# Finer projection parts, placed by a table around the row pieces of a causal attention stage

## The reference

```
q = concat(heads(x @ Wq1), heads(x @ Wq2))     # 16 + 16 heads of 32 columns, two inputs x [1024, 512] each
k2, v2 = repeat(heads(x @ Wk), 2), repeat(heads(x @ Wv), 2)
p = softmax(where(causal, q @ k2.T / sqrt(32), min))
y1, y2 = split(p @ v2)
x = x + (y1 - sigmoid(x @ Wlam) * y2) @ Wo
```

## Time and profile before

| what | value |
|---|---|
| median of 3 runs | 2034.17 us (2033.46 to 2034.27) |
| the profiled execution | 2035.76 us |
| its span, first to last instruction | 2034.0 us |
| everything ahead of the attention's prologue | 0 to about 760 us |
| attention prologue | 760 to 815 us |
| units 0 to 15 | 815 to 1669 us |
| last feed-forward layer | 1669 to 2034 us |
| TensorE busy over the span | 1962.1 us, 96% |
| VectorE, GpSimd, ScalarE busy over the span | 64%, 42%, 41% |

### The profile page before, as it was taken

The page is one execution under the profiler, slowest core; times in us unless marked ns, Lnnn a source line. Parts: engine busy times, 40 slices in busy tenths (PEclk is TensorE's granted clock), DMA queues, the critical chain, the costliest instruction groups (busy, mean ns, idle before and its releaser), DMA issues.

```text
span 2034.0 us, 36832 instructions
## 1 busy us (share of the span) xinstructions
PE 1962.1 (96%) x15143; PEld 834.2 (41%) x15184; DVE 1305.1 (64%) x2610; ACT 827.7 (41%) x1259; POOL 864.2 (42%) x451
## 2 busy tenths in 40 slices
PE   7898999899999999999999999999998899899999
PEld 3444444444444443333333333333333334344444
DVE  5878686846847456566666666666667635774644
ACT  4435353425444322444434443344434452543431
POOL 3756576700000000667677667777776740000000
PEclk9999999999999999999999999999999999999999
DMA  8111010030000003000101010010000211000001
GB/s 243 32 31 33 30 42 27 21 140 1 1 1 1 1 1 76 23 17 23 22 22 22 12 26 14 22 23 22 2 22 6 60 36 42 1 1 22 21 0 42
DMA packets 71592, 60.21 MB, mean 30 GB/s; under 512 B 37312, under 2 KB 55744, under 8 KB 71168
## 3 DMA queue, kind: packets, MB, share of 16 engines
q1 hardware_dynamic: 64512, 45.27, 8.0%
q10 hardware_dynamic: 6912, 12.59, 2.0%
HBM read 43.02 MB, written 10.62 MB: 26 GB/s over the span
## 4 chain that ended last, share of the span: by engine, by line
PE 53%; DVE 5%; POOL 2%; issue 1%; ACT 1%; DVEq 0%; POOLq 0%; ACTq 0%
PE psum L128 9%; PE psum L1231 8%; PE psum L1321 8%; PE psum L1379 6%; PE psum L1362 6%; PE psum L152 5%; PE psum L1271 3%; PE psum L1335 2%; PE psum L1358 2%; POOL b_totals L1628 1%; PE psum L1349 1%; DVE b_maxima L1701 1%; PE psum L1280 1%; DVE psum L1709 1%; DVE x L1767 0%
## 5 line engine op out<-in xcount | busy, mean ns | idle before, releaser
L1628 POOL TENSOR_TENSOR b_totals<-b_totals,b_probs 128x2048 f32<-128x2048 f32 (+3 forms) x100 | 323.9, 3239 | 151.7 <-ACT b_probs L1546 148.1
L1709 DVE CUSTOM_DVE_ANT_0 psum<-psum,b_rest 128x512 f32<-128x512 f32 (+3 forms) x512 | 233.7, 526 | 172.2 <-PE psum L1321 172.0
L447 PE MATMUL psum<-hT,a_win 128*128 128x512 f32 x640 | 292.9, 601 | 2.6 <-DVE a_parts L751 1.2
L128 PE MATMUL psum<-hT,b_early 128*128 128x512 f16 x1024 | 227.2, 381 | 9.8 <-DVE b_middle L214 6.9
L128 PE MATMUL psum<-hT,W 128*128 128x512 f16 x1024 | 227.5, 382 | 3.7 <-DVE a_win L214 3.6
L1546 ACT ACTIVATE b_probs<-psum 128x1024 f32<-128x1024 f32 (+3 forms) x214 | 153.6, 768 | 150.5 <-PE psum L1362 150.4
L1701 DVE TENSOR_REDUCE b_maxima<-psum 128x2 f32<-128x1024 f32 x128 | 150.9, 1221 | 86.0 <-PE psum L1321 85.7
L1628 POOL TENSOR_TENSOR b_totals<-b_totals,b_rest 128x2048 f32<-128x2048 f32 (+3 forms) x50 | 161.9, 3238 | 68.3 <-ACT b_rest L1546 66.6
L447 PEld LDWEIGHTS psum<-hT,a_win 128*128 128x128 f32 x640 | 120.2, 192 | 130.8 <-issue 129.5
L128 PEld LDWEIGHTS psum<-hT,b_early 128*128 128x128 bf16 x1024 | 100.0, 98 | 133.8 <-DVE b_middle L214 8.8
L128 PEld LDWEIGHTS psum<-hT,W 128*128 128x128 bf16 x1024 | 100.7, 99 | 126.4 <-issue 7.0
(11 more groups left out here) (244 smaller groups left out, 3476.6 us busy)
## 6 DMA issues: line engine op xcount, KB each, us to landing
a_parts<-in_w_guT ACTq DMA_DIRECT2D x32, 256.0 KB, 2.7
ternary<-W SPq DMA_DIRECT2D x1, 6144.0 KB, 18.3
a_win<-in_w_inT SPq DMA_DIRECT2D x20, 256.0 KB, 7.9
a_parts<-in_w_pT ACTq DMA_DIRECT2D x16, 256.0 KB, 2.6
b_down<-lam_rows SPq DMA_DIRECT2D x32, 128.0 KB, 2.7
b_early<-ternary SPq DMA_DIRECT2D x8, 512.0 KB, 8.9
out<-x SPq DMA_DIRECT2D x16, 256.0 KB, 2.3
x<-in_x SPq DMA_DIRECT2D x3, 1024.0 KB, 8.0
```

What stands on the lines that cost most here:

```text
L128: last = pe.matmul(self.bank[self.up_bank(i, m) + part], self.gu[:, k * 2 * HID + col:k * 2 * HID + col + P], self.hT[:, at:at + BLK], sta ...
L447: last = pe.matmul(ring(s, j), win[:, at:at + P], core["hT"][:, (i * KT + k) * BLK:(i * KT + k + 1) * BLK], start=(k == 0), stop=(k == KT ...
L1628: pool.tensor_tensor(acc, acc, held(u, s)[:, :, off:BLK], ALU.add).then_inc(summed, 1)
L1709: last = dve.tensor_tensor_reduce(scores, scores, row_mask[:, BLK - width:BLK], 1.0, -3e38, ALU.add, ALU.max, maxima[u % 2][:, at:at + 1])
```

## The change

1. A "k" or "q" job now has 8 parts of half the width: the parts 0 to 3 do the first 256 token columns over the four input blocks, the parts 4 to 7 the other 256. A "v" job also has 8 parts, of 4 matmuls where it had 4 of 8. A unit with four jobs has 32 parts, of half the size.
2. A step has 6 places in place of 2. Places 0 and 1 come ahead of the rows, 2 to 5 behind. Two tables say how many parts stand in a step, `AHEAD_OF_ROWS` and `BEHIND_ROWS`. The sums over the next chunk of queries move: "den1" from behind the rows of step 2 to ahead of the rows of step 3, "den0" to place 3 of step 5, which is behind one part of a projection.
3. The row pieces stand in another order.
4. In unit 14, where "norm" jobs take the place of the projections, all four stand behind the rows; the one of step 4 stood ahead.

```diff
-ROWS = [[(0, 0), (2, 0)], [(4, 0)], [(1, 0), (5, 1)], [(5, 0)], [(6, 0)], [(4, 1), (6, 1)], [(3, 0)], [(7, 1)], [(7, 0)]]
+ROWS = [[(4, 0)], [(5, 0)], [(0, 0), (2, 0)], [(1, 0), (5, 1)], [(3, 0)], [(4, 1), (6, 1)], [(6, 0)], [(7, 1)], [(7, 0)]]
...
-PARTS = {"k": KT, "q": KT, "v": KT}
+PARTS = {"k": 2 * KT, "q": 2 * KT, "v": 2 * KT}
 
-FIRST_HALF = {(0, 0): "k0", (2, 1): "den1", (3, 0): "k1", (5, 1): "den0", (6, 0): "q0", (8, 0): "q1", (10, 1): "neg0"}
-SECOND_HALF = {(0, 0): "q0", (2, 1): "den1", (3, 0): "q1", (5, 1): "den0", (6, 0): "v0", (8, 0): "v1", (10, 1): "neg0"}
+MADE_IN = [("k0", "k1", "q0", "q1"), ("q0", "q1", "v0", "v1")]
+AHEAD_OF_ROWS = {4: 2, 5: 1, 6: 1, 7: 1, 8: 1}
+BEHIND_ROWS = {0: 2, 1: 3, 2: 3, 3: 1, 4: 3, 5: 1, 6: 3, 7: 3, 8: 3, 9: 4}
+PLACES = 6
+FILLS = []
+for _names in MADE_IN:
+    _halves = [(i, first + n) for i in range(NS) for first, table in ((0, AHEAD_OF_ROWS), (2, BEHIND_ROWS))
+               for n in range(table.get(i, 0))]
+    FILLS.append({at: _names[n // (2 * KT)] for n, at in enumerate(_halves)})
+    FILLS[-1].update({(3, 0): "den1", (5, 3): "den0", (10, 2): "neg0"})
...
-FILL_BEFORE_ROWS = (0, 4)
-NORM_AT = {(3, 0): 0, (4, 0): 1, (6, 0): 2, (7, 0): 3}
+NORM_AT = {(3, 2): 0, (4, 2): 1, (6, 2): 2, (7, 2): 3}
...
-            def project(weights, r, c, k, to):
-                at = ((r // HT * CQ + c) * KT + k) * BLK
+            def project(weights, r, c, part, to):
+                k, width = part % KT, BLK // 2
+                first = part // KT * width
+                at = ((r // HT * CQ + c) * KT + k) * BLK + first
                 for own in COLUMNS:
-                    last = pe.matmul(to[own, :], weights[:, k * P + own.start:k * P + own.stop], hT[:, at:at + BLK],
-                                     start=(k == 0), stop=(k == KT - 1))
+                    last = pe.matmul(to[own, first:first + width], weights[:, k * P + own.start:k * P + own.stop],
+                                     hT[:, at:at + width], start=(k == 0), stop=(k == KT - 1))
...
-                    if i in FILL_BEFORE_ROWS and (u, i, 0) in PART_AT:
-                        fill(*PART_AT[u, i, 0])
-                    if row_in(u, i):
-                        row(*row_in(u, i))
-                    if i not in FILL_BEFORE_ROWS and (u, i, 0) in PART_AT:
-                        fill(*PART_AT[u, i, 0])
-                    if (u, i, 1) in PART_AT:
-                        fill(*PART_AT[u, i, 1])
+                    for place in range(PLACES):
+                        if place == 2 and row_in(u, i):
+                            row(*row_in(u, i))
+                        if (u, i, place) in PART_AT:
+                            fill(*PART_AT[u, i, place])
```

More of the change, by code:

```diff
@@ L1 @@
+import itertools
 from contextlib import ExitStack
@@ L940, in job_from @@
         return {(1, 1): ("den", u - 1, 1), (4, 0): ("den", u, 0)}.get((i, place))
-    name = (SECOND_HALF if w else FIRST_HALF).get((i, place), "none0")
+    name = FILLS[w].get((i, place), "none0")
     kind, n, last = name[:-1], int(name[-1]), r == TURNS - 1
@@ L964 @@
 EPILOGUE_BANKS = [7]
-PLACES = [(u, i, place) for u in range(UNITS) for i in range(NS) for place in range(2)]
 PART_AT, ENDING, STEADY = {}, {}, []
-for _n, _at in enumerate(PLACES):
+for _at in itertools.product(range(UNITS), range(NS), range(PLACES)):
     _job = job_from(*_at)
     if _job:
[L971 to L976, removed]
+        if not STEADY or STEADY[-1] != _job:
+            STEADY.append(_job)
+            _part = 0
+        PART_AT[_at] = (_job, _part)
+        _part += 1
+        if _part == PARTS.get(_job[0], 1):
+            ENDING[_at] = _job
 JOBS = PROLOGUE + STEADY + EPILOGUE
@@ L1266, in fill @@
                     pe.wait_ge(wv_loaded, 16)
[L1267 to L1274, removed]
+                    t, k = 2 * two + part // KT, part % KT
+                    at = ((b * CQ + t // TPB) * KT + k) * BLK + t % TPB * P
+                    for own in COLUMNS:
+                        last = pe.matmul(to[own, t % 2 * 2 * P:(t % 2 + 1) * 2 * P],
+                                         hT[:, at + own.start:at + own.stop],
+                                         wv_all[:, k * D + h * P:k * D + (h + 2) * P],
+                                         start=(k == 0), stop=(k == KT - 1))
                 elif kind == "den":
@@ L1558, in _ @@
                         weigh_out(u - 1, 1)
-                    if i == CHUNK_LAST[0] + 1:
-                        weigh_out(u, 0)
                     if u == UNITS - 2 and i == 0:
@@ L1563, in _ @@
                         act.activation(e_root[:, :], e_var[:, :], ACT.Sqrt).then_inc(early_root, 1)
-                    for place in range(2):
+                    for place in range(PLACES):
                         if (u, i, place) in ENDING:
                             copy_out(ENDING[u, i, place])
+                        if place == 0 and i == CHUNK_LAST[0] + 1:
+                            weigh_out(u, 0)
             weigh_out(UNITS - 1, 1)
@@ L1819, in _ @@
                 for i in range(NS):
-                    if u == UNITS - 2 and NORM_AT.get((i + 1, 0), 2) < 2:
-                        early_turn(0, NORM_AT[i + 1, 0])
+                    if u == UNITS - 2 and NORM_AT.get((i + 1, 2), 2) < 2:
+                        early_turn(0, NORM_AT[i + 1, 2])
                     if i == NS - 2 and u + 1 < UNITS:
```

## The result

| | median | lowest to highest | executions |
|---|---|---|---|
| before | 2034.04 us | 2033.46 to 2034.27 | 4 |
| after | 2053.99 us | 2052.18 to 2054.57 | 4 |

The change makes the kernel slower by 1.0%: the ratio of the times is 1.0097, with a 95% interval of 1.0081 to 1.0113. The forecast was 2056, 2 us too high, with the range of 2039 to 2063 around it. The profiled execution of after took 2052.18 us, the shortest of its four, and its span is 2050.4 us.

What follows compares the result with a forecast made beforehand. TensorE, busy 96% at full clock, bounds the kernel. Per steady unit 3.27 us added less 1.59 removed is +1.68, 21.8 over 13 units; unit 0 +1.15, unit 14 0, prologue -0.75 make +22.2: 2056 us, range 2050 to 2063, 2039 with partial rivals.

Steps and rivals of the forecast that it cites:

- removed, step 3: scores: Steady unit, step 3: the scores' second bank pair waits for VectorE, with a "den" behind the rows before; 0.35 us goes.
- removed, steps 5 and 6: scores: Steady unit, start of steps 5 and 6: scores stall on VectorE's first reduction without showing idle time; 0.37 us each goes.
- removed, rows of steps 7 and 8: Rows' second pair waits for the first pair's exponential; one small part ahead of the rows covers 0.25 us in each.
- added, step 1: Step 0 loses two small parts, so step 1's `weigh` must wait for the copy of bank 6: 0.31 us, units 1 to 13.
- added, step 4: Step 4's scores follow masked rows and one small part, 1.60 us against 2.88: 1.25 us stall, the largest new term.
- added, step 5: Step 5's scores follow step 4's masked rows with 2.53 us of work against 2.88: 0.33 us stall.
- added, round trip: Step 5: "den" follows a job's last part in the same bank and waits for ScalarE's copy; 0.85 us (0.67 to 0.98).
- The yardstick: Time from rows' start until scores get their second bank pair: 2.45 us plain, 2.88 masked pair, 2.65 one masked 512.
- the rival that had it free: Step 5's wait of "den" is hidden by ScalarE or the queue ahead: 12 us less, 2044 us; chance 0.06.
- The rival that the clock falls in each unit: Two gaps of some 0.9 us in each unit bring TensorE's clock to half: about 2098 us; chance 0.05.
- the rival "faster": Step 4's scores and step 5's "den" find their banks free: 1.17 us new against 1.59 removed, about 2028 us; chance 0.08.
- the rival "small parts cost": Halved projection parts cost what the skill's rule says, 1.8 us on each of 48 jobs: about 2140 us; no chance given.

Runs made afterwards that it cites:

- the run without the round trip: The change, with step 5's projection part from behind the rows moved ahead of them, so the rows stand before "den": 2051.55 us, ratio 1.0086.
- the better order: The changed kernel with tables edited: masked rows where most parts stand behind, plain rows where few do, "den" behind rows: 2028.61 us, ratio to before 0.9966.
- the kernel with step 1's stall filled: The change, with one small part moved from behind the rows of step 2 into step 0: 2057.92 us, ratio 1.0116.
- the exchanged pieces: The table with masked rows where most parts stand behind, with row pieces (7, 0) and (7, 1) swapped in `ROWS`: 2026.63 us, ratio 0.9963.
- the kernel with VectorE's plain reduction: The change, with step 3's row pieces reduced without their mask, two plain reductions per pair for four masked: 2046.71 us, ratio 1.0065.

## Why the prediction was right, point by point

| step of the prediction | forecast | measured in unit 4 |
|---|---|---|
| removed, step 3: scores | 0.35 | 0.35 (1.15 to 0.80) |
| removed, steps 5 and 6: scores | 0.37 each | step 6: 0.37 (1.57 to 1.20); step 5 see below |
| removed, rows of steps 7 and 8 | 0.25 each | 0.25 each (1.32 and 1.33 to 1.07 and 1.08) |
| added, step 1 | 0.31 | 0.27 |
| added, step 4 | 1.25 | 1.20 (1.20 to 2.40) |
| added, step 5 | 0.33 | 0.34 |
| added, round trip | 0.85 | 0.83 |
| added, step 7 | 0.37 | 0.34 (1.20 to 1.54) |
| added, step 9 | 0.16 | 0.13 |
| a steady unit | +1.68 | +1.63 |

In step 5 the old stall went and the new one came, so that its scores take 1.54 us where they took 1.56; the two terms are seen as a sum only. The kernel with the new places and the old rows has step 5 without either, at 1.20 us.

**The yardstick** carried the forecast. It said when a bank pair comes free by the row's start and the kind of reduction, and each of its three numbers came back: 2.88 twice in the change, 2.64 in the run without the round trip, 2.46 in the better order.

**Halving costs nothing.** The run with short parts alone has 0.9996 of the time before. The Trainium skill ("TensorE: Matmul & The Clock Gate", Back-to-back issue gap) would have given some 85 us, an estimate from its figures for 128 and 512 columns; this case disagrees, and its jobs of 256 and 512 columns take 3.66 and 3.64 us.

**The round trip** was 0.80 to 0.83 us, by what a small part is taken to cost, for 0.85, so the rival that had it free falls, as do the ones with the stall of step 4 absent, with the time falling and with nothing moved. The rival that the clock falls in each unit falls too: units 0 to 13 have a mean of 1.00 although each has an idle 0.72 us.

**Mis-sized terms.** The prologue gave 0.90 us for 0.75. It starts 0.64 us earlier as well, which I hadn't costed: 0.72 of that is there before the attention's first job, in code that the change doesn't touch, and the four jobs at once take 14.02 for 13.94 us. Unit 0 cost 1.26 for 1.15 (50.65 to 51.91).

**Unit 14 is where the sum missed.** I took 0, from a gain by the plain first rows and a loss by the norms. It measured -2.20, just outside its bounds, and the reason isn't one that I had weighed: in the change's profile the clock does not fall there. The prediction wrote the fall down as something that the wait for ScalarE in step 1 brings along. In the kernels below it is there in some and not in others. Where the clock does fall under the change's instructions for unit 14 (the kernel with step 1's stall filled), the unit takes 57.10 us, 0.56 more than before's 56.54 at the same mean of 0.94, and that is inside the bounds.

**Two slips that change nothing.** In the rival "faster" 14 units at 1.59 less 1.17 are 5.9 us and not 5.5, and the rival "small parts cost" was given a time but no chance.

**The 2 us that are left.** The span grew by 16.4 us for a forecast of 22.2. Unit 14 and the last layer, both with a fall of the clock in before's profile and none in after's, are 3.9 us of that. Most of this belongs to the two executions that were profiled: the medians differ by 19.95 us. The forecast less what was too dear in the units (0.66), too little in the prologue (0.15), the earlier start (0.64) and unit 15 (0.50), and with the 0.56 of unit 14 at the same clock, is 20.8. So the terms of units 0 to 13 carried the median, and 0.8 us stay unaccounted for.

## What to carry to other kernels

- When bank pairs rotate between a producer and a reducer, find for each kind of reduction the time from the producer's start to the moment the bank is free (here 2.45, 2.65 and 2.88 us), and let at least that much work, the producer's own included, pass before the bank is wanted. Put the long fills behind the slow reductions; work moved between two slow ones only moves the stall.
- Two jobs that share a bank need something between them as long as the copy's round trip (here 1.35 us from the first job's start). Taking a wait away is worth only its distance to the next one: 0.92 us, of which 0.8 was waiting, gave 0.37.
- Read stalls of array-shared matmuls from start to start. The change lost 1.2 us a unit in a place where the profile has no idle time.

## What the runs showed that I had not expected

The length of unit 14 hangs on TensorE's granted clock, and this differs between kernels whose instructions in unit 14 are the same. The windows of unit 14 of the change stand above (54.34 us at 1.00). Those of the kernel with the stall of step 1 filled, the whole unit and 14 us from its step 1 on:

```profile
1600.67:1657.77 57.10, 50.62 (x534) 18.40 (x529) 38.78 (x97) 25.81 (x35) 42.60 (x19) 0.94 0.27 84
1604.00:1618.00 14.00, 11.21 (x107) 3.49 (x104) 5.88 (x7) 6.39 (x10) 6.38 (x3) 0.76 0.00 1
```

A mean of 0.76 over 14 us is 6.7 us at the lower of the two levels, 1.2 GHz, the rest at 2.4. The same stretch of the change:

```profile
1603.00:1617.00 14.00, 10.90 (x136) 4.06 (x134) 7.53 (x10) 7.65 (x12) 7.91 (x4) 1.00 0.01 1
```

The unit is 57.10 against 54.34 us, 2.8 us for 6.7 us at half. The kernel with three parts moved out of step 4 has 57.11 at 0.94 and the one without the round trip 56.94 at 0.94, both with the unit's instructions unchanged. What TensorE did before the fall is the same in both cases, a wait for ScalarE in step 1. In the change, where the clock stays:

```profile
1605.07 1.13 PE L1330 MATMUL psum<-b_middle 32*128 32x512 f32 x4
1607.72 1.13 PE L1330 MATMUL psum<-b_middle 32*128 32x512 f32 x4 [1.52 <-ACT b_rest L1552]
```

The kernel before waits longer at this place, 2.16 us, since its first rows are the narrow ones of 0.49 us, and there the clock fell:

```profile
1584.33 0.49 PE L1321 MATMUL psum<-b_middle 32*128 32x128 f32 x4
1586.97 1.70 PE L1321 MATMUL psum<-b_middle 32*128 32x128 f32 x12 [2.16 <-ACT b_rest L1546]
```

In the profiles of all five kernels with the 2.16 us the clock fell to half in this unit, and of the six with 1.52 us it fell in four. With one profile of each kernel that is no more than a hint that the shorter wait spares it at times. In three profiles, those of the new order in the old places, of the three parts moved out of step 4 and of the exchanged pieces, it fell in unit 13 too (mean 0.97). What decides it stays open.

The executions of one kernel differ in the same way. Of the kernel with VectorE's plain reduction three took spans of 2044.8 and 2044.9 us at a mean clock of 0.997, and the fourth 2049.5 at 0.995. So executions are best compared at the same mean clock. Those of before that ran beside the experiments with a mean of 0.997 have spans of 2031.0 to 2032.5 us, 2031.95 on average; the change's two at 0.997 have 2052.5 and 2052.8. That is 20.7 us, and it says that the 16.4 us between the two profiles are no measure of the change alone. The last feed-forward layer fits: before has a mean of 0.79 over 8 us of it, which is 3.4 us at the lower level, and the change, without that fall, was 1.65 us shorter there with the same code.

```profile
1735.00:1743.00 8.00, 5.67 (x18) 2.39 (x19) 2.49 (x4) 3.16 (x5) 0.00 (x0) 0.79 0.00 0
```
